# Unread bf16 products in five places of the middle stage of a six-stage network

## The reference

```
x = x + 0.5 * L0_ffn(layernorm(x))    # two layers of local attention (window 64) and a gated feed-forward
x = x + L0_attn(layernorm(x))         # eight heads with relative positions
x = x + 0.5 * L0_ffn(layernorm(x))
x = x + 0.5 * L1_ffn(layernorm(x))    # 64 experts, the best 8 of each token
x = x + L1_attn(layernorm(x))         # state-space layer: convolution, 16 states, a scan over tokens
x = x + 0.5 * L1_ffn(layernorm(x))
```

```
Q, K, V = q @ w_qs * scale, q @ w_ks, q @ w_vs          # split into 8 heads of 128
attn = einsum(Q + rel_embed_bias, K)
attn_pos = relative_shift(einsum(Q + rel_pos_bias, positions @ w_rel_pos_k))
out = einsum(softmax(attn + attn_pos), V) @ w_out + b_out
```

## Time and profile before

| | us |
|---|---|
| median of 3 timed runs | 4794.54 |
| lowest and highest | 4786.48, 4795.5 |
| the profiled execution | 4797.14 |
| its span, first to last instruction | 4795.1 |
| TensorE busy | 3971.9 (83%) |
| VectorE busy | 3014.1 (63%) |
| ScalarE busy | 2772.1 (58%) |
| GpSimd busy | 2071.1 (43%) |
| mean granted TensorE clock | 0.933 of full speed |

### The profile page before, as it was taken

How to read it: one execution, slowest core, us unless ns; L and a number is a source line. 1 busy time by engine, 2 the same in 40 slices (tenths; PEclk the granted TensorE clock), 3 DMA queues, 4 the chain that set the end, 5 groups by cost and what they waited for, 6 DMA issues and landing times. The chain is left out here.

```text
span 4795.1 us, 54417 instructions
## 1 busy us (share of the span) xinstructions
PE 3971.9 (83%) x17076; PEld 2403.6 (50%) x17076; DVE 3014.1 (63%) x5743; ACT 2772.1 (58%) x6174; POOL 2071.1 (43%) x1350
## 2 busy tenths in 40 slices
PE   6787898888888888888987989878888888888846
PEld 3445554555545554455544555445554555445412
DVE  4326666667576674766657666666757667477464
ACT  4466557565576565665566655756557556565332
POOL 2104254544364441744436434454436444175334
PEclk9799999999999999999999999999999999999867
DMA  3020013111131111210121101311113111121212
GB/s 104 1 90 1 17 56 115 36 48 37 38 123 39 38 46 60 93 49 25 59 87 61 55 29 54 112 38 49 34 42 123 39 38 46 60 90 52 78 49 76
DMA packets 188824, 274.01 MB, mean 57 GB/s; under 512 B 23448, under 2 KB 102900, under 8 KB 188532
## 3 DMA queue, kind: packets, MB, share of 16 engines
q1 hardware_dynamic: 186340, 268.72, 17.6%
q10 hardware_dynamic: 2192, 1.70, 0.1%
HBM read 215.54 MB, written 54.79 MB: 56 GB/s over the span
## 5 line engine op out<-in xcount | busy, mean ns | idle before, releaser
L604 POOL TENSOR_TENSOR work<-work 128x512 f32<-128x512 f32 x512 | 667.9, 1305 | 1211.9 <-DVE work L664 1124.3
L1515 POOL TENSOR_TENSOR work<-work,minus_half 128x8 f32<-128x8 f32 x256 | 473.9, 1865 | 537.2 <-DVE work L1498 534.2
L664 DVE SCALAR_TENSOR_TENSOR work<-work,psum 128x512 f32<-128x512 f32 x528 | 362.3, 687 | 419.6 <-ACT work L596 418.6
L1618 ACT ACTIVATE work<-psum,work 128x128 f32<-128x128 f32 (+1 forms) x1024 | 392.6, 397 | 387.8 <-DVE work L1640 387.4
L572 PE MATMUL psum<-work,w_up 128*128 128x512 f32 x1024 | 545.6, 616 | 64.2 <-DVE work L664 60.4
L596 ACT ACTIVATE work<-psum 128x512 f32<-128x512 f32 x528 | 315.9, 599 | 434.1 <-PE psum L572 427.0
L578 PE MATMUL psum<-work,w_down 128*128 128x512 f32 x1024 | 542.3, 612 | 3.4 <-POOL work L604 3.4
L1443 PE MATMUL psum<-wqkv,xn 128*128 128x512 f32 x768 | 389.4, 634 | 56.0 <-PEq L387 39.4
L1583 PEld LDWEIGHTS psum<-work 128*128 128x128 f32 x3072 | 388.9, 197 | 61.3 <-issue 47.9
L1583 PE MATMUL psum<-work 128*128 128x64 f32 x3072 | 412.0, 279 | 9.2 <-ACT work L1605 8.6
L1572 PE MATMUL psum<-ident,work 128*128 128x128 f32 x1536 | 250.3, 288 | 151.9 <-ACT work L1618 116.4
(11 more groups left out here) (238 smaller groups left out, 8476.5 us busy)
## 6 DMA issues: line engine op xcount, KB each, us to landing
work<-expert_weight_rows SPq DMA_DIRECT2D x1024, 128.0 KB, 2.9
position_scores<-work SPq DMA_DIRECT2D x64, 768.0 KB, 3.5
work<-position_scores SPq DMA_DIRECT2D x64, 512.0 KB, 3.8
work<-state_readout_rows SPq DMA_DIRECT2D x72, 256.0 KB, 4.4
rows<-state_readout_rows SPq DMA_DIRECT2D x32, 256.0 KB, 4.0
sq<-state_readout_rows SPq DMA_DIRECT2D x24, 256.0 KB, 4.2
rows<-in_L_attn_q SPq DMA_DIRECT2D x8, 256.0 KB, 3.6
expert_weight_rows<-work SPq DMA_DIRECT2D x16, 128.0 KB, 2.3
```

The lines of the kernel that those rows point to most:

```text
L604: pool.tensor_tensor(h, h, self.weights[p % self.SLOTS], ALU.mult).then_inc(self.gated, 1)
L664: v.scalar_tensor_tensor(out=self.gate_h[p % 3][0:rows], in0=self.tanh_h[p % self.turns][0:rows], scalar=1.0, in1=bank(b, self.ups[p % sel ...
L1515: pool.tensor_tensor(half, half, b.minus_half[:].broadcast_to([128, LH]), ALU.pow).then_inc(self.inv_norm, 1)
L1618: ins = self.nc.scalar.activation(out[:, x, -n:] if t else out[:, x], self.scores(m)[:, x], ACT.Exp, bias=self.neg_max[i % 2][:, slot:slot ...
```

## The change

Five calls of `keep_busy` are added in `attn_stage`, and two calls are divided so that one can stand between their halves: the guest's steps up to 3 into up to 2 and up to 3, and the last norm into its two products. Nothing that is read changes. The banks are 3 (free until the first output projection) and 7 (the scores' bank, free after the last head).

```diff
             beside.tensor(pe)
             norm.tensor(pe, b.x[:], (0, 1), steps=(1,))
+            beside.tensor(pe, upto=2)
+            keep_busy(nc, b, 3, 14)
             beside.tensor(pe, upto=3)
             pe.wait_ge(norm.done, 1)
...
             queries_keys(0)
             beside.tensor(pe, upto=5)
+            keep_busy(nc, b, 3, 8)
             distances(0, (0, 1, 2, 3))
+            keep_busy(nc, b, 3, 8)
             for i in range(ROUNDS):
...
                 beside.tensor(pe, upto=so_far(i, 3))
+            keep_busy(nc, b, 7, 8)
             pe.wait_ge(x_done, 1)
-            after.tensor(pe, b.x[:], (0, 2))
+            after.tensor(pe, b.x[:], (0, 2), steps=(0,))
+            keep_busy(nc, b, 7, 4)
+            after.tensor(pe, b.x[:], (0, 2), steps=(1,))
+            keep_busy(nc, b, 7, 16)
```

## The result

| | before | after |
|---|---|---|
| median, us | 4795.02 (8 runs) | 4818.39 (8 runs) |
| lowest and highest | 4786.48, 4805.05 | 4806.91, 4823.33 |
| the profiled execution | 4797.14 | 4818.07 |
| ratio of times, 95% interval | 1 | 1.0038 [1.0022, 1.0053] |

The change is slower by 0.38%, 18 us with an interval of 10.5 to 25. (The two medians of the table are 23.4 us apart, in the upper part of that interval; the text goes by the ratio.) Set on the median that the prediction started from, that is 4813 [4805, 4820]. The forecast's sum was +7.8 us, so the sign of the sum is right and its size is less than half of what was measured.

The account below looks back on a forecast made before the run. No engine alone bounds the middle stage, a chain hopping between engines. Seven guest stages at +0.98 (0.33 + 1.73 + 0.62 - 1.7) and one at +0.95 gave +7.8 us: 4802 on the median, range 4786 to 4814, the forecast's own 4795 to 4810.

Parts of the forecast that it names:

- The chain: Middle stage, run eight times: no engine bounds it alone, work hops between engines; the change makes it about 2.7 us longer.
- No cost at the distance scores: Rival, chance 0.10: something else is as late as ScalarE's copies, so products ahead of first distance scores are free; 4789.
- The third stage's start: Products behind the last norm remove the 1.2 GHz stretch; the next stage's first eight records take 3.6 us: -1.7 a stage.
- Edit 3: Eight products after the first distance scores: cost 0, because ScalarE is still copying and reads the next result later.
- the eight of edit 4: Eight products before `x_done`, ahead of the last norm, make it 0.62 us late per stage; 5 us in all.
- Edits 4 and 5: Last norm, eight products before, four inside, 16 behind: +0.62 and -1.7 us per stage, about 9 us faster.
- Edit 1: 14 products behind the guest's squares: L787 0.33 us late per stage, no clock regained; 2.6 us slower in all.
- Edit 2: Eight products before the first distance scores, where TensorE does not wait: +1.73 us per stage, 13.8 us in all.
- A moved stretch: Later stages' 1.2 GHz stretches may strike work or a wait: 0 to 1.7 us each, no net effect taken.
- slower: Rival, chance 0.15: the added products themselves run at 1.2 GHz in half of the stages, +12 us more, 4814.
- The whole low stretch counts: Rival, chance 0.06: each stage regains 3.3 us instead of 1.7, as waits inside the stretch hang on slowed matmuls; 4790.
- faster: Rival, chance 0.16: low stretches shift into waits, so L1068 and products at the stage's start run at 2.4 GHz; 4780.

Follow-up runs that it names:

- dist8: Kernel before plus only eight unread products ahead of the first distance scores: 1.0043 [1.0026, 1.0059], 20.6 us slower.
- dist16: Kernel before plus only 16 unread products ahead of the first distance scores: 1.0057 [1.0042, 1.0072], 27 us slower.
- dist24: Kernel before plus only 24 unread products ahead of the first distance scores: 1.0075 [1.0060, 1.0090], 36 us slower.
- after8: Kernel before plus only eight products behind the first distance scores: 0.9995 [0.9984, 1.0006].
- end8: Kernel before plus only the eight products ahead of the last norm: 1.0015 [1.0002, 1.0028], +7 us.
- end28: Kernel before plus eight products ahead of the last norm, four between its two products, 16 behind it: 1.0009 [0.9998, 1.0020], +4 us.
- last16: Kernel before plus four products between the last norm's two products and 16 behind it: 0.9981 [0.9968, 0.9994], -9 us.
- norm14: Kernel before plus only 14 products behind the guest's squares: 0.9982 [0.9970, 0.9994], -8.6 us.
- no_dist: The changed kernel less the eight products ahead of the first distance scores, against the kernel before: 0.9983 [0.9970, 0.9997], -8 us.
- control: The kernel before, unchanged, timed and profiled once more against itself: 1.0001 [0.9986, 1.0016].
- filled: Kernel before plus 12 products behind guest's squares, 4 and 16 at last norm, 8 behind V products, 16 in second distance-score round: 0.9948 [0.9929, 0.9967], -25 us.

## Why the prediction was right or wrong

- **The chain.** Right. The profile shows the four signs that it named: 1.73 us more at the distance scores with ScalarE waiting, the last norm 0.6 to 0.7 later, the third stage's start at 1.00 with 3.76 us for eight records (3.6 said), and the middle stage 2.67 us longer (2.7 said, in part by luck, as told above). L787 was 0.42 later (0.33 said). In the stage without a guest the 14 products took 3.96 us (4.5 said) and the V products 7.03 (7.0 said).
- **"No cost at the distance scores"** is refuted by dist8, dist16 and dist24: +21, +27 and +36 us.
- **The third stage's start.** Right: -1.7 forecast, -1.69 in the profile. The Trainium skill (TensorE: Matmul & The Clock Gate, Terms) would give 3.3 for the 6.6 us stretch, an estimate by its factor of one half; the measured start bears out the smaller value, since half of the stretch lay in a wait. Over whole executions it is 0.26 us for each us of low time, again about half of that factor.
- **Edit 3 at nothing and the eight of edit 4 at 5 us.** Right, by after8 and end8. Edits 4 and 5 together were forecast at -9 and gave +4 [-1, 10]. The -1.7 at the third stage's start is there, but the low time of end28's executions fell by 17 us only, where eight stretches of 6.6 us would be 53, and its profile has low stretches at three other stages' starts. Why they come with the 28 products and not with the 20 of last16 stays open.
- **Edit 1.** The sign is wrong: +2.6 forecast, -8.6 measured. The step that failed is "The clock there is back at 2.4 GHz by then, so nothing is regained". It was read from one profile in which no stage was hit there. norm14's executions spend 25 us less at 1.2 GHz than those of the kernel before, an estimated -6.6 us, which with the +2.6 gives -4, inside the measured [-14, -3]. Where the time is regained, no profile shows.
- **Edit 2, +13.8, is the term that was mis-sized.** It is one of three that were off, and the other two, edit 1 by -11 us and edits 4 and 5 by +13, nearly cancel; so it is edit 2 that leaves the sum of 7.8 below the interval of 10.5 to 25. In the change it is 26 ± 10 us; alone it cost 20.6 [12.5, 28.3], which leaves room for 13.8. The products' own 0.216 each stands. What comes on top is in part seen in the profiles: in dist8 the low stretch strikes L787 in five stages. In the change the stretch behind the DMA wait begins one matmul earlier (L1062's pair takes 1.65 us instead of 0.91) and lasts 6.8 us in six of seven stages, and from the distance scores to the first scan it is 21.8 to 21.9 us there. In no_dist it lasts 3.4 us in five of seven, and the way is 21.1. That is some 0.75 x 6 = 4.5 us. Over all executions the change has 23 us more of low time than no_dist (-33 against -56 in the table), an estimated 6 us, and 13.8 + 6 = 20 lies within 26 ± 10. Why the eight products lengthen the stretch is not shown.
- **"A moved stretch can strike work or a wait: 0 to 1.7 us each, and I take no net effect."** This was named as the exposed point, and it is where the three measured terms (edit 1, edit 2, edits 4 and 5) part from the forecast by 7 to 13 us each. In one profile 15.0 of the 21.0 us lie in code without an edit, but the control moves by half of that by itself, so a profile cannot settle it.
- **The rivals.** The measured time is near that of "slower" (4814), but its mechanism was not seen: of the 464 added products in the change's profile five ran at 1.2 GHz, all in the stage without a guest. "The whole low stretch counts" is refuted by the -1.69 of the third stage's start. The mechanism of "faster", 1.2 GHz kept off the first scores and the stage's start, is real. The change did not reach it, because edits 2 and 3 leave the wait behind the DMA open; filled does reach it, with -25 us.

The single edits add up to -8.6 + 20.6 - 2.4 + 4.3 = +14 ± 12 us, and 18 [10.5, 25] were measured for the whole, so the parts may add up; a joint effect of some us is not excluded. The time lies in the range of 4786 to 4814, near its upper end, and that by the cancelling of two errors.

## What to carry to other kernels

In this kernel unread products pay only in a wait that they don't outlast, ahead of work whose end others wait for. So ask of each place first whether TensorE waits there, and only then what the clock would give: the same eight products cost 20 us above a line and nothing below it. Price each place in a run of its own: one bad place in five hid a gain of 8 us. When an effect is some tenths of a per cent, read from the profile the stretches around the edit, leave the total to repeated timings, and look at the mean clock of all of them: it told here what no single profile could.

## What was not expected

The stretches at 1.2 GHz do not stay with the waits that bring them. In fourteen profiles of thirteen kernels whose instructions are the same up to the first middle stage, that stage began after 236.6 to 246.3 us. In the nine without products ahead of L787, the stretch from the norm to the first queries took 18.8 to 20.5 us in 50 of 63 stages and 22.4 to 23.1 in the other 13. Filling the longest wait took the low stretch away behind it: from the distance scores to the first scan filled needs 20.24 us on average, the other kernels 21.0 to 22.4.

No forecast had what one place does to the clock elsewhere: eight products ahead of the first distance scores added 48 us of low time to dist8's executions, and 16 or 24 at the same place -2 and +9.
